# The other two edits, and two late row pairs turned and summed inside the last cross attention

## The chip, the cores and the metric

One NeuronCore of a Trainium2 chip. The metric is device time in microseconds (us) of one execution, as the median of several. TensorE (PE) does the matmuls, VectorE (DVE), ScalarE (ACT) and GpSimd (POOL) the rest, and SyncE (SP) issues all transfers between HBM and SBUF. Each engine works through its own list of instructions in order and waits on semaphores.

## The reference

A decoder layer with pre-norm, x of 4 x 512 x 1024 in f32:

```python
x = x + self_attention(layernorm(x))           # 32 heads of 32, 16 KV heads, causal, with biases
x = x + cross_attention(layernorm(x), ctx)     # 32 heads, 8 KV heads, 64 context rows, a mask
xn = layernorm(x)
g, u = xn @ Wg.T, xn @ Wu.T                    # NF4 codes x absmax per 64 columns, 3584 x 1024
x = x + (silu(g) * u) @ Wd.T                   # NF4 as well, 1024 x 3584
```

## The kernel before

Matmuls work on f16 pairs: a value is a high part and a low part, and a product takes three matmuls (high x high, high x low, low x high). ScalarE writes the high (a copy), VectorE or POOL the low (value minus high).

**Attention.** Self attention runs in steps s = -6 to 67. A step scores one block (`score`), turns and weighs another, and projects q, k or v in four pieces (`project`, L1164, L1170). Steps -6 to -3 only project; step -2 is the first that also scores, and needs masks which POOL writes (L1060 to L1077) and counts in `selected`. Projections go through HBM (`nat_parts`) into `q_rows` and `k_rows`. The last batch's cross attention comes by itself (`last_cross`), 16 iterations n and a tail. An iteration is a chain: PE score (L1259), VectorE mask and maximum (L1671, L1675), POOL shift (L996), ScalarE exponential (L1440), PE turn (L1266), ScalarE high (L1444), VectorE low (L1679), PE weigh (L1278), VectorE output `x_out` (L1684, L1688), POOL add (L1003).

**The FFN's input.** It is 1024 columns x 2048 rows, worked on as eight row pairs j. Pairs 0 to 3 are made during self attention. For each late pair 4 to 7: SP loads (L292), VectorE takes statistics (L301 to L307), POOL the root (L312), VectorE normalises (`normal`, L321), PE turns in two phases (L336), ScalarE copies (L345), VectorE makes five sums (`sum_turned`, L359), and ScalarE and POOL cut seven highs (L370) and seven lows (L376, counted in `x_low`).

**Gate and up.** Quadrants are multiplied by a seven-product scheme (Strassen and Winograd): M1 to M7 of 12 matmuls each make a *set* (L2081), 56 sets s = 2k + nb for k = 0 to 27. Set 0 can run on the first pairs, set 1 needs all of them (`x_low` 56). During half step (k, nb) the other engines dequantise two tiles of k + 1's weights: ScalarE draws codes and their comparisons (`draw`, L425 in part 0, L428), VectorE looks them up (L438, six times) and subtracts (L449), POOL scales (L455), sums (L465) and cuts lows (L482), ScalarE cuts highs (L478). The hidden values go through HBM in f16 pairs.

**Down.** 28 chunks of two tiles each, in slabs of 3, 4, 7, 7 and 7 chunks; each slab passes over all 16 rows of 128, with six matmuls 128x512 per chunk and row (L2114). `add_down` (L2339) adds a row's two banks to y. A down tile is drawn, looked up and scaled as above, then `down_high` (ScalarE, L2143) and `down_low` (POOL, L1988) cut it. The six tiles of slab 0 are made in k = 27's half steps, three each, those of slab s + 1 during slab s (`tiles_in`), spread over its 16 rows. Three pairs of PSUM banks take turns for the rows. SP loads h rows (L1935, seven slots) and, at the slab's start, the 16 rows of y (L1940).

## Time and profile before

| | us |
|---|---|
| median of 3 runs | 2695.02 (2693.35 to 2696.4) |
| span of the profiled execution | 2699.7 |
| PE busy in it | 2469.7 (91%) |
| DVE busy | 1786.3 (66%) |
| ACT busy | 1631.8 (60%) |
| POOL busy | 1525.4 (57%) |

The profile describes one execution, whose span is 4.7 us above the median of the runs; durations below are its own. Line numbers are those of the kernel before. A row "10.77 <-POOL" says that the engine stood idle for 10.77 us ahead of this instruction and that POOL ended it.

### The profile page before, as it was taken

To read this page: it belongs to the slowest core of one execution; us is meant where nothing else is said; L and a number is where in the kernel's file an instruction comes from. 1 tells how busy PE (TensorE), PEld (TensorE's weight loads), DVE (VectorE), ACT (ScalarE), POOL (GpSimd) and SP (SyncE) were. 2 spreads that over 40 slices of the span, in tenths; PEclk is the share of its full clock that TensorE was granted. 3 is DMA by queue.
4 is the path that set the end of the run, shared out by engine and by line. 5 is a ranking of instruction groups with operands and counts; after the bars stand their busy time and mean duration, and the time that the engine had idled before them with its cause. 6 is when DMAs were issued, how large, how long until landed. Compare 5 with 4: busy or idle time off the path is not lost.

```text
span 2699.7 us, 48588 instructions
## 1 busy us (share of the span) xinstructions
PE 2469.7 (91%) x17864; PEld 1343.9 (50%) x17864; DVE 1786.3 (66%) x3004; ACT 1631.8 (60%) x2998; POOL 1525.4 (57%) x1360
## 2 busy tenths in 40 slices
PE   5899999999985557999999999999997897999999
PEld 3576777777764333444444444444443333444444
DVE  5566678767777766777777777777777666555511
ACT  3466666666665436777777777777775565544400
POOL 2356677777769456777777777777774222222200
PEclk9999999999987568999999999999998998999999
DMA  6243443433232211322222222222325433333232
GB/s 199 81 141 108 119 130 105 121 108 107 80 103 87 77 48 43 90 90 88 89 91 82 83 90 83 89 86 86 93 86 202 139 106 114 105 99 100 93 103 76
DMA packets 225885, 271.11 MB, mean 100 GB/s; under 512 B 37616, under 2 KB 148720, under 8 KB 225648
## 3 DMA queue, kind: packets, MB, share of 16 engines
q1 hardware_dynamic: 225648, 268.00, 31.7%
q8 instruction: 143, 2.34, 0.4%
q14 instruction: 94, 0.77, 0.1%
HBM read 192.81 MB, written 73.40 MB: 99 GB/s over the span
## 4 chain that ended last, share of the span: by engine, by line
PE 49%; DVE 3%; issue 3%; POOL 3%; ACT 2%; DMA 1%; SPq 0%; DVEq 0%; POOLq 0%; ACTq 0%
PE ps L2081 33%; PE ps L2114 16%; POOL xT L455 1%; DVE ps L438 1%; ACT w_l L428 1%; DVE p L438 1%; DVE xT L449 1%; DMA proj<-in_codes 1%; ACT ps L425 1%; POOL xn L1993 0%; POOL q_rows L482 0%; SPq L1940 0%; DMA h_parts<-xn 0%; POOL p L465 0%; POOL x_row L1999 0%
## 5 line engine op out<-in xcount | busy, mean ns | idle before, releaser
L438 DVE TENSOR_TENSOR ps<-ps,w_l 128x512 f32<-128x512 f32 x672 | 443.0, 693 | 283.7 <-ACT w_l L428 157.3
L455 POOL TENSOR_TENSOR xT<-xT,nat 128x512 f32<-128x512 f32 x164 | 208.9, 1274 | 530.5 <-DVE xT L449 530.5
L982 POOL TENSOR_TENSOR arena<-p,arena 128x512 f16<-128x512 f32 x320 | 371.1, 1168 | 225.8 <-ACT arena L1436 225.1
L428 ACT ACTIVATE w_l<-proj 128x512 f32<-128x512 int32 x672 | 397.8, 616 | 9.4 <-DMA proj<-in_codes 9.4
L1428 ACT ACTIVATE p<-ps 128x512 f32<-128x512 f32 x320 | 191.1, 597 | 265.7 <-PE ps L1223 260.8
L1640 DVE TENSOR_REDUCE block_max<-ps 128x4 f32<-128x512 f32 x320 | 219.2, 688 | 182.5 <-PE ps L1194 179.9
L2081 PE MATMUL ps<-arena,q_rows 128*128 128x512 f16 x1344 | 296.4, 380 | 10.5 <-POOL arena L376 10.3
L425 ACT ACTIVATE ps<-proj,small 128x512 f32<-128x512 int32 x336 | 216.9, 677 | 90.2 <-DVE xT L449 87.2
L2339 DVE SCALAR_TENSOR_TENSOR arena<-ps,arena 128x1024 f32<-128x1024 f32 x70 | 84.9, 1221 | 241.2 <-PE ps L2114 230.0
L1164 PE MATMUL ps<-xT,w_h 128*128 128x512 f16 x720 | 222.0, 391 | 10.8 <-POOL arena L1077 10.8
L2081 PEld LDWEIGHTS ps<-arena,q_rows 128*128 128x128 f16 x1344 | 131.8, 98 | 170.7 <-POOL arena L376 10.8
L1436 ACT ACTIVATE arena<-p 128x512 f16<-128x512 f32 x320 | 192.0, 620 | 0.0
L2081 PE MATMUL ps<-w_h,q_rows 128*128 128x512 f16 x840 | 191.5, 383 | 0.0
L465 POOL TENSOR_TENSOR p<-xT 128x512 f32<-128x512 f32 x135 | 171.9, 1274 | 10.3
L2114 PE MATMUL ps<-w_h,w_l 128*128 128x512 f16 x672 | 150.6, 381 | 9.8 <-POOL w_h L1988 6.3
L1192 PE MATMUL ps<-k_rows,q_rows 96*128 96x512 f16 (+3 forms) x512 | 136.6, 306 | 21.0 <-DMA q_rows<-nat_parts 11.0
L2081 PE MATMUL ps<-arena,k_rows 128*128 128x512 f16 x672 | 152.0, 379 | 1.4 <-DVE x_row L2294 1.4
L1221 PE MATMUL ps<-q_rows,k_rows 97*128 97x512 f16 (+3 forms) x512 | 136.8, 306 | 13.6 <-DVE arena L1679 9.5
L1164 PE MATMUL ps<-xT,w_l 128*128 128x512 f16 x360 | 140.5, 390 | 0.0
L2081 PEld LDWEIGHTS ps<-w_h,q_rows 128*128 128x128 f16 x840 | 83.2, 99 | 100.9 <-issue 4.3
L2154 ACT ACTIVATE x_row<-ps 128x512 f32<-128x512 f32 x110 | 64.7, 588 | 105.4 <-DVE xT L2265 34.7
L449 DVE TENSOR_TENSOR xT<-ps,p 128x512 f32<-128x512 f32 x164 | 113.4, 692 | 5.7
(246 smaller groups left out, 5951.4 us busy)
## 6 DMA issues: line engine op xcount, KB each, us to landing
proj<-in_codes SPq DMA_DIRECT2D x168, 256.0 KB, 2.6
nat<-in_scales SPq DMA_DIRECT2D x336, 128.0 KB, 2.9
h_parts<-xn SPq DMA_DIRECT2D x112, 256.0 KB, 2.3
nat_parts<-nat SPq DMA_DIRECT2D x48, 256.0 KB, 2.0
q_rows<-nat_parts SPq DMA_DIRECT2D x96, 128.0 KB, 2.7
w_l<-h_parts SPq DMA_DIRECT2D x21, 448.0 KB, 4.1
x_unit<-in_x SPq DMA_DIRECT2D x64, 128.0 KB, 2.7
x<-x_unit SPq DMA_DIRECT2D x64, 128.0 KB, 2.4
```

The source lines that it names most:

```text
L425: op = self.nc.scalar.activation(out, self.t.codes[:, t % 2, :], ACT.Relu, scale=slope, bias=(self.t.above, self.t.below)[side])
L428: op = self.nc.scalar.activation(out, self.t.codes[:, t % 2, :], ACT.Copy, scale=slope, bias=intercept)
L438: self.nc.vector.tensor_tensor(other if n == self.LUT - 2 else held, held, other, ALU.max).then_inc(self.lut, 1)
L455: self.nc.gpsimd.tensor_tensor(self.quarter(t), self.quarter(t), self.t.scales[:, t % 2, :], ALU.mult)\
L465: self.nc.gpsimd.tensor_tensor(self.w_sum(k, m), self.quarter(4 * k + a), self.quarter(4 * k + b), op)\
L982: nc.gpsimd.tensor_tensor(p_l[:, n % 2, k, :], p32[:, f % 3, :], p_h[:, n % 2, k, :], ALU.subtract).then_inc(p_low, 1)
L1164: mm = nc.tensor.matmul(dst[:, :], w[:, c, cols], xT[:, :, half, c, :], start=(c == 0 and m == 0), stop=(c == CT - 1 and m == 2))
L1428: nc.scalar.activation(p32[:, f % 3, :], bank[T_BANK + T_OF[f % CHUNKS]][:, :], ACT.Exp, scale=SELF_SCALE).then_inc(t_exp, 1)
L1436: nc.scalar.activation(p_h[:, n % 2, k, :], p32[:, f % 3, :], ACT.Copy).then_inc(p_high, 1)
L1640: nc.vector.reduce_max(block_max[:, n % PAIRS, k, :], bank[S_BANK + S_OF[k]][:, :].rearrange("p (a n) -> p a n", n=P), AX_X)\
L2081: mm = nc.tensor.matmul(out, t.fw[k % 2][m][:, w, P * c:P * c + P], feed.x_of(nb, m, x, c), start=(n == 0 and m in (M1, M2, M3, M6)), stop ...
L2114: mm = nc.tensor.matmul(ps[:, 2 * (idx % 3) + half, :], hT[:, n, h, :], d[:, w, HALF * half:HALF * half + HALF], start=(n == 0 and m == 0) ...
```

## The change

It has four parts.

1. *Startup.* The wait for all masks moves from ahead of step -6 to ahead of step -2, and step -2's four projection pieces are issued ahead of its scores.
2. *Late pairs 4 and 5* are handled inside `last_cross`: pair 4's statistics in n = 9, normal 10, turn and sums 11 and 12, highs and lows from 12 to 15; pair 5's statistics in 13, normal 14, turn and sums 15 and 16, highs and lows behind. Sums now lie in the tails of `k_rows` and `q_rows` for all late pairs, copies in `x1T`; the first cut of k = 1's weights therefore waits for all 56 lows. PE's turn of iteration n - 1 comes before the weigh of n - 2.
3. *Down tiles.* Two of them (`EARLY`, chunk 0) are made as a third tile in half steps (23,0) and (25,0); k = 27 makes two in each half step. Later slabs' tiles are spread over 14 rows. ScalarE writes a tile's high between the two parts of the next tile's draws.
4. *The start of the down matmul.* h rows 0 to 3 are loaded before the last half step; y is loaded one row at a time beside h and the tiles.

```diff
@@ tensor, attention
-        pe.wait_ge(selected, 8)
         for s in range(FROM, TO):
+            if s == -2:
+                pe.wait_ge(selected, 8)
             step(s)
...
+            if s == -2:
+                for piece in range(4):
+                    project(kind_in(s), piece)
             for k in range(CHUNKS):
...
-                if kind_in(s) is not None and k < 4:
+                if kind_in(s) is not None and k < 4 and s != -2:
                     project(kind_in(s), k)
@@ last_cross
+                if 1 <= n <= NX:
+                    if n >= 2:
+                        pe.wait_ge(x_low, x - 1)
+                    x_turn(x - 1, LT_BANK, p32[:, (x - 1) % 3, :])
                 if n >= 2:
...
                     x_weigh(x - 2, LO_BANK, p_h[:, x % 2, 0, :], p_l[:, x % 2, 0, :])
-                if 1 <= n <= NX:
-                    if n >= 2:
-                        pe.wait_ge(x_low, x - 1)
-                    x_turn(x - 1, LT_BANK, p32[:, (x - 1) % 3, :])
...
+                if n in (11, 12, 15, 16):
+                    feed.turn(pe, 4 + n // 15, (n + 1) % 2 if n >= 15 else n - 11)
@@ scalar, last cross
+            if n in (11, 15):
+                for half in range(2):
+                    feed.copy_turned(act, 4 + n // 15, half)
...
+            for high in {12: (0, 1, 2), 13: (3, 4), 14: (5, 6)}.get(n, ()):
+                feed.x_cut_high(act, 4, high)
@@ gpsimd, last cross
+            for low in {12: (0, 1), 13: (2, 3), 14: (4,), 15: (5, 6)}.get(n, ()):
+                feed.x_cut_low(pool, 4, low)
@@ gpsimd, feed forward
-        x_lows(4, range(4))
         feed.root(pool, 6)
-        x_lows(4, range(4, 7))
-        x_lows(5, range(7))
+        x_lows(5, range(4))
+        feed.root(pool, 7)
+        x_lows(5, range(4, 7))
+        x_lows(6, range(3))
         join(0)
-        feed.root(pool, 7)
-        x_lows(6, range(7))
+        x_lows(6, range(3, 7))
         x_lows(7, range(7))
@@ cut_high
+        if k == 1:
+            act.wait_ge(self.x_low, 56)
@@ tiles
+    EARLY = (NK - 5, NK - 3)
...
         if k + 1 < NK:
-            return [4 * (k + 1) + 2 * nb, 4 * (k + 1) + 2 * nb + 1]
-        return [WT + 3 * nb + n for n in range(3)]
+            early = [feed.down_tile(feed.EARLY.index(k))] if nb == 0 and k in feed.EARLY else []
+            return [feed.weight_tile(k + 1, 2 * nb), feed.weight_tile(k + 1, 2 * nb + 1)] + early
+        return [feed.down_tile(len(feed.EARLY) + 2 * nb + n) for n in range(2)]
@@ sync, down
+                if (k, nb) == (NK - 1, 1):
+                    for idx in range(4):
+                        load_h(idx)
...
+        for n in range(4):
+            load_y(n)
+            store_h(8 * GROUPS - 4 + n)
+            if 4 + n < H_SLOTS:
+                load_h(4 + n)
         for idx in range(NI):
+            if idx + 4 < RT:
+                if idx + 4 == 14:
+                    sp.wait_ge(h_low, 8 * GROUPS)
+                load_y(idx + 4)
@@ scalar, down
-        for idx in range(NI):
-            for at in tiles_in(idx):
-                feed.draw(act, at, 0)
-                feed.draw(act, at, 1)
-                down_high(at)
...
+        for before, at in zip(LATE, LATE[1:]):
+            feed.draw(act, at, 0)
+            down_high(before)
+            feed.draw(act, at, 1)
+        down_high(LATE[-1])
```

Where rows move, in order. First, VectorE in the last cross attention (after the change L349 is `sum_turned`; L1671 to L1688 and L1709 to L1726 are an iteration's softmax and output, L301 to L307 and L294 to L300 statistics). Before, in the last iterations:

```order
L1671 TENSOR_TENSOR p<-ps,arena 128x512
L1675 TENSOR_REDUCE s_top<-p 128x8
L1679 TENSOR_TENSOR arena<-ps,arena 128x512
L1684 RECIPROCAL rx_sum<-ps 128x8
L1688 TENSOR_TENSOR arena<-ps,rx_sum 128x256
L1679 TENSOR_TENSOR arena<-ps,arena 128x512
L1684 RECIPROCAL rx_sum<-ps 128x8
L1688 TENSOR_TENSOR arena<-ps,rx_sum 128x256
L301 BN_STATS arena<-xn 128x6 x2
L304 BN_AGGR f_moments<-arena 128x2
L307 TENSOR_SCALAR f_moments<-f_moments 128x1
```

After, in n = 12 and 13:

```order
L1722 RECIPROCAL rx_sum<-ps 128x8
L1726 TENSOR_TENSOR arena<-ps,rx_sum 128x256
L349 TENSOR_TENSOR k_rows<-ps,x1T 128x512 x3
L349 TENSOR_TENSOR q_rows<-ps,x1T 128x512
L1709 TENSOR_TENSOR p<-ps,arena 128x512
L1713 TENSOR_REDUCE s_top<-p 128x8
L1717 TENSOR_TENSOR arena<-ps,arena 128x512
L1722 RECIPROCAL rx_sum<-ps 128x8
L1726 TENSOR_TENSOR arena<-ps,rx_sum 128x256
L294 BN_STATS arena<-xn 128x6 x2
L297 BN_AGGR f_moments<-arena 128x2
L300 TENSOR_SCALAR f_moments<-f_moments 128x1
```

Four of pair 4's sums now stand ahead of an iteration's softmax, where there were none. Pair 5's statistics (the last three rows) come behind the softmax of n = 13 and no longer between the last low part and the last output.

Second, ScalarE in the late tiles (L425 and L428 draw; after the change L436 and L439; L2143 and L2199 are `down_high`). Before:

```order
L2143 ACTIVATE w_h<-xT 128x512
L428 ACTIVATE w_l<-proj 128x512 x2
L425 ACTIVATE ps<-proj,small 128x512 x2
L428 ACTIVATE w_l<-proj 128x512
L428 ACTIVATE nat<-proj 128x512
L428 ACTIVATE w_l<-proj 128x512
L428 ACTIVATE p<-proj 128x512
L2143 ACTIVATE w_h<-xT 128x512
```

After:

```order
L439 ACTIVATE w_l<-proj 128x512 x2
L436 ACTIVATE ps<-proj,small 128x512 x2
L2199 ACTIVATE w_h<-xT 128x512
L439 ACTIVATE w_l<-proj 128x512
L439 ACTIVATE nat<-proj 128x512
L439 ACTIVATE w_l<-proj 128x512
L439 ACTIVATE p<-proj 128x512
```

The high now comes after the first four draws of the next tile, and no longer between two tiles.

Third, SP at the end of the gate and up matmuls (L1920, after the change L1967, stores the hidden values; L1935 and L1982 load h rows; L1940 and L1987 load y). Before:

```order
L411 DMA nat<-in_scales 64x512 x2
L406 DMA proj<-in_codes 128x512
L411 DMA nat<-in_scales 64x512 x2
L1935 DMA w_l<-h_parts 128x768 x3
L1920 DMA h_parts<-xn 128x4x256 x4
L1940 DMA arena<-x 128x1024 x4
L1935 DMA k_rows<-h_parts 128x768 x2
L1935 DMA x1T<-h_parts 128x768
L1935 DMA x_row<-h_parts 128x768
L1940 DMA arena<-x 128x1024 x10
L1940 DMA xT<-x 128x1024 x2
L406 DMA proj<-in_codes 128x512
```

After:

```order
L417 DMA proj<-in_codes 128x512
L422 DMA nat<-in_scales 64x512 x2
L1967 DMA h_parts<-xn 128x4x256 x2
L417 DMA proj<-in_codes 128x512
L422 DMA nat<-in_scales 64x512 x2
L1987 DMA arena<-x 128x1024
L1967 DMA h_parts<-xn 128x4x256
L1982 DMA k_rows<-h_parts 128x768
L1987 DMA arena<-x 128x1024
L1967 DMA h_parts<-xn 128x4x256
L1982 DMA k_rows<-h_parts 128x768
L1987 DMA arena<-x 128x1024
```

The h loads come first, and a single row of y stands between a store and an h load, where four and then ten were sent at once.

## Rows read from the trace of the kernel before

**Rows 1.** Stretches: PE, PEld, DVE, ACT, POOL busy (instructions), PEclk, DMA share, GB/s.
```profile
0.00:110.00 110.00, 72.45 (x535) 43.11 (x536) 58.01 (x91) 39.15 (x56) 26.20 (x37) 0.94 0.49 159
...
780.00:990.14 210.14, 118.95 (x1160) 89.80 (x1157) 159.16 (x309) 105.15 (x195) 142.81 (x141) 0.66 0.23 71
990.14:1048.20 58.06, 33.03 (x148) 18.92 (x149) 32.91 (x54) 28.63 (x51) 36.69 (x33) 0.76 0.08 28
1048.20:2052.72 1004.52, 1000.71 (x4620) 451.11 (x4620) 740.76 (x1165) 765.52 (x1419) 730.27 (x602) 1.00 0.28 87
2052.72:2148.16 95.44, 70.56 (x307) 30.11 (x307) 63.44 (x88) 47.93 (x87) 30.28 (x25) 0.91 0.60 202
2148.16:2265.72 117.56, 94.34 (x403) 40.24 (x403) 79.57 (x114) 69.59 (x127) 33.98 (x28) 0.92 0.35 107
```

**Rows 2.** Startup's timelines: start, duration, engine, line, [idle before <-releaser].
```profile
32.74 1.03 PE L1164 MATMUL ps<-xT,w_h 128*128 128x512 f16 x2 [10.77 <-POOL arena L1077]
...
40.37 0.59 PE L1164 MATMUL ps<-xT,w_h 128*128 128x512 f16 x2
...
50.73 0.28 PE L1170 MATMUL ps<-w_h,xT 128*128 128x128 f16 x2
...
62.41 0.61 PE L1192 MATMUL ps<-k_rows,q_rows 96*128 96x512 f16 x1 [4.59 <-DMA q_rows<-nat_parts]
...
22.64 0.69 DVE L1594 TENSOR_TENSOR xT<-ps,xT 128x512 f16<-128x512 f32 x1 [0.16 <-ACT xT L1369]
...
24.72 2.45 DVE L1546 SCALAR_TENSOR_TENSOR w_l<-x_row,w_h 128x1024 f16<-128x1024 f32 x2
```

**Rows 3.** Timeline of ScalarE in the last cross attention.
```profile
967.74 0.63 ACT L1440 ACTIVATE p<-p 128x512 f32<-128x512 f32 x1 [0.47 <-POOL p L996]
...
971.53 0.63 ACT L1440 ACTIVATE p<-p 128x512 f32<-128x512 f32 x1 [0.47 <-POOL p L996]
...
978.11 0.63 ACT L1440 ACTIVATE p<-p 128x512 f32<-128x512 f32 x1 [3.25 <-POOL p L996]
```

**Rows 4.** Timelines of the FFN's head.
```profile
995.79 0.32 SPq L292 DMA_DIRECT2D xn<-x  x1
...
990.36 1.09 PE L336 MATMUL ps<-ident,xn 128*128 128x128 f32 x4 [3.14 <-issue]
...
991.53 0.80 DVE L321 TENSOR_SCALAR x_unit<-x_unit,f_moments 128x1024 f32<-128x1024 f32 x1
...
1016.70 1.64 DVE L321 TENSOR_SCALAR x_unit<-x_unit,f_moments 128x1024 f32<-128x1024 f32 x1
...
1007.27 12.09 POOL L376 TENSOR_TENSOR arena<-arena 128x512 f16<-128x512 f32 x10
...
1048.20 14.72 PE L2081 MATMUL ps<-arena,q_rows 128*128 128x512 f16 x60 [10.30 <-POOL arena L376]
...
1067.53 1.17 POOL L482 TENSOR_TENSOR q_rows<-p,q_rows 128x512 f16<-128x512 f32 x1
```

**Rows 5.** Timelines of the start of the down matmul.
```profile
2065.59 13.31 PE L2114 MATMUL ps<-q_rows,w_l 128*128 128x512 f16 x54 [12.87 <-issue]
...
2075.11 1.23 DVE L2339 SCALAR_TENSOR_TENSOR arena<-ps,arena 128x1024 f32<-128x1024 f32 x1 [11.15 <-DMA arena<-x]
```

**Rows 6.** Timelines of slab 1 of the down matmul.
```profile
2168.34 1.91 DVE L438 TENSOR_TENSOR ps<-ps,w_l 128x512 f32<-128x512 f32 x3 [2.59 <-ACT ps L425]
...
2166.06 0.63 ACT L2143 ACTIVATE w_h<-xT 128x512 f16<-128x512 f32 x1 [3.17 <-POOL xT L455]
...
2173.04 15.70 PE L2114 MATMUL ps<-w_h,w_l 128*128 128x512 f16 x72
```

**Rows 7.** Timelines of the last k's two half steps.
```profile
2039.48 2.75 PE L2081 MATMUL ps<-arena,k_rows 128*128 128x512 f16 x12 [1.35 <-DVE x_row L2294]
...
2055.35 1.91 DVE L438 TENSOR_TENSOR ps<-ps,w_l 128x512 f32<-128x512 f32 x3 [0.76 <-ACT ps L425]
```

**Rows 8.** TensorE's waits, 1060 to 2045 us: total, times, longest.
```profile
PE ps L2081 <- POOL q_rows L482: 2.3, 2, 1.8
```

More of the change, by code:

```diff
@@ L441, in subtract @@
         dve.wait_ge(self.lut, self.LUT * t + self.LUT - 1)
-        k, j = t // 4, t % 4
-        if 8 <= t < self.WT + 4:
+        d = self.down_index(t)
+        early = len(self.EARLY)
+        k, j = self.weight_index(t) if d is None else (self.NK, d % 4)
+        if d is None and k >= 2 or d is not None and early <= d < early + 4:
             dve.wait_ge(self.w_summed, 5 * (k - 1) + (3, 5, 4, 5)[j])
@@ L446, in subtract @@
                 dve.wait_ge(self.w_low, 7 * (k - 1) + (None, 2, 4)[j])
-        elif t >= self.WT + 4:
-            dve.wait_ge(self.d_low, t - 4 - self.WT + 1)
+        elif d is not None and 1 <= d < early:
+            dve.wait_ge(self.d_low, d)
+        elif d is not None and d >= early + 4:
+            dve.wait_ge(self.d_low, d - 3)
         self.nc.vector.tensor_tensor(self.quarter(t), self.maximum(0), self.line(t, 1, 3), ALU.subtract)\
@@ L962, in _ @@
             sp.wait_ge(x2_stored[x1_slot(rt)], 16 * x1_count(B - 2, rt))
+        sp.wait_ge(ln_turned, 2 * LN_AT["cross", B - 1, 2] + 2)
+        feed.load_pair(sp, 4)
         sp.wait_ge(ln_turned, 2 * len(LN_ORDER))
-        for j in range(4, 6):
-            feed.load_pair(sp, j)
+        feed.load_pair(sp, 5)
         store_last(1)
@@ L1897, in tiles_in @@
         lo, hi = 2 * SLAB_AT[s + 1], 2 * SLAB_AT[s + 2]
-        return [WT + lo + n for n in range((hi - lo) * r // RT, (hi - lo) * (r + 1) // RT)]
+        ends = [min(hi, lo + (hi - lo) * n // (RT - 2)) for n in (r, r + 1)]
+        return [feed.down_tile(d) for d in range(*ends)]
+    LATE = [at for idx in range(NI) for at in tiles_in(idx)]
     def h_tile(i, nb, c):
@@ L2035, in half_step @@
                 down_low(tiles[0])
-                feed.scale(pool, tiles[2])
                 down_low(tiles[1])
-                down_low(tiles[2])
+            else:
+                for at in tiles[2:]:
+                    feed.scale(pool, at)
+                    down_low(at)
         def x_lows(j, ns):
@@ L2054, in _ @@
                 half_step(k, nb)
-        for n in range(8 * GROUPS - 4, 8 * GROUPS):
+        for n in range(8 * GROUPS - 4, 8 * GROUPS - 1):
             hidden_low(n)
-        for idx in range(NI):
-            for at in tiles_in(idx):
-                feed.scale(pool, at)
-                down_low(at)
+        for n, at in enumerate(LATE):
+            feed.scale(pool, at)
+            if n == 0:
+                hidden_low(8 * GROUPS - 1)
+            down_low(at)
     @block.tensor
@@ L2119, in _ @@
         rest.banks_free(pe)
-        turn(4)
         pe.wait_ge(x_low, 28)
@@ L2133, in down_high @@
         def down_high(at):
-            chunk = (at - WT) // 2
+            d = feed.down_index(at)
+            chunk = d // 2
             act.wait_ge(feed.scaled, at + 1)
-            if chunk < 3:
+            if chunk < 1:
+                pass
+            elif chunk < 3:
                 act.wait_ge(product, 7 * (NSET - 2))
@@ L2208, in half_step @@
                 down_high(tiles[0])
-                for part in range(2):
-                    feed.draw(act, tiles[2], part)
                 down_high(tiles[1])
-                down_high(tiles[2])
+            else:
+                for at in tiles[2:]:
+                    feed.draw(act, at, 0)
+                    feed.draw(act, at, 1)
+                    down_high(at)
             if s >= 1 and k % 2 == 0:
@@ L2226, in _ @@
         act.wait_ge(w_low, 7)
-        copies(4)
-        highs(4, range(2))
+        highs(5, range(3))
         copy(0, 0)
-        highs(4, range(2, 7))
+        highs(5, range(3, 7))
         copy(0, 1)
-        copies(5)
-        highs(5, range(7))
         copies(6)
@@ L2236, in _ @@
         copies(7)
+        highs(7, range(7))
         rest.scores_done(act)
@@ L2323, in half_step @@
             feed.subtract(dve, tiles[1])
-            if k + 1 == NK:
-                look_up(tiles[2])
+            for at in tiles[2:]:
+                look_up(at)
             if s >= 1:
```

151 lines of the change are left out of this document (81 added, 70 removed).

## The prediction

> **What bounds the kernel now.** I read the table of stretches first [rows 1]: where is TensorE not busy? From 1048.20 to 2052.72 us (sets 1 to 55 of the FFN) it is busy 1000.71 of 1004.52 us. It is the bound there, and an edit can only cost time. It stands still for 37.6 us before 110, for 91.2 in the last cross attention (780 to 990.14), for 25.0 in the FFN's head (to 1048.20), and for 24.9 and 23.2 in the first two slabs of the down matmul (2052.72 to 2265.72). A gain has to come out of these gaps.
>
> Second, the timelines at the gaps, for what each wait is charged to:
> - Startup [rows 2]. The first projection starts at 32.74, after 10.77 us charged to a POOL memset. What it computes with was there long before: the last activations (VectorE L1594, 22.64 + 0.69 = 23.3) and the fourth low part of the weights (L1546, 27.2). Later a score waits 4.59 us for q_rows.
> - Last cross attention [rows 3]. The exponentials of two steps are 3.8 us apart where VectorE has only the softmax (967.74, 971.53), and 6.6 where it also has pair 4's statistics (971.53, 978.11).
> - The FFN's head [rows 4]. 58.06 us pass from the end of the last cross attention (990.14) to set 1 (1048.20). POOL decides: ten of its lows run from 1007.27, and set 1 waits 10.30 us for its last.
> - Down matmul [rows 5, 6]. Set 55 ends at 2052.72, the first down matmul starts at 2065.59 after 12.87 us, and the first add waits 11.15 us for a row of y that was sent in a burst. Slab 1 advances by VectorE's dequantisation, 14 tiles in its 117.56 us [rows 1], some 8 us each. VectorE waits 2.59 us of it for ScalarE's draw (L425, ahead of 2168.34), and ScalarE, ahead of its high (L2143), 3.17 us for POOL's scale.
>
> **Term 1, startup.** Without the wait for the masks, the first projection starts at 23.4 instead of 32.74, -9.3. It took 7.63 us (to 40.37 [rows 2]), at first on the lower clock. Started at 23.4, its last quarter comes after 28, when the fourth low part (27.2) is there, so nothing new waits. And the four pieces of the next projection now stand ahead of the first scores. From the end of q2's matmuls (50.73, two projections after 40.37, so 5.18 each) to the score that waits for q_rows (62.41) a chain of 11.7 us runs through bias, stores and SP; TensorE filled it with v and then stood still for 4.59. With 5.2 us of projection in that place the wait is covered. What is lost is that these pieces no longer fill later waits for VectorE's maxima. I take -4.2 of the 4.6: **-13.5** (-10 to -15).
>
> **Term 2, last cross attention and head.** The last cross attention ends later. VectorE gets ten sums of 128x512 f32; three operations of that shape take 1.91 us [rows 6], so 6.4 us. TensorE gets four turn phases, each of two groups like that of 1.09 us at 990.36 [rows 4], 8 us in all, where it is busy 118.95 of 210.14 us. Against that TensorE now turns step n-1 before it weighs step n-2, so the exponentials' chain no longer has the weighing in it: some 0.5 us of a clean step of 3.8, over twelve steps 6 at most. Pair 5's statistics no longer stand right ahead of the last x_out, four sums do. I take +4.4 (+2 to +8).
>
> After it, the head. Pair 6's load is issued at 995.79, when pair 4 has been turned (990.36 and on) [rows 4]; now pair 4 was turned before, and only the last store is ahead, so the rows land some 5 us after the end of attention instead of 9. Then some 3 us of statistics (6.6 - 3.8 in [rows 3], rounded up), 0.7 of root, and on POOL 21 lows at 1.21 (12.09 for ten) and 2 us of join and root: 5 + 3 + 0.7 + 25.4 + 2 = 36.1, so some 37 instead of 58.06, -21. TensorE's own 33.03 us there fall by the four phases, so it isn't the bound. But k = 1's weights don't come earlier by as much: the two silus now stand ahead of ScalarE's first draw for them, and its first cut waits for all 56 lows, since the sums lie in its room. POOL's M1 low (1067.53 + 1.17) was done just when set 2 began, 20 us after set 1. A lag of 3 us against little slack is a stall of 2 to 3. Sum: 4.4 - 21 + 2.6 = **-14** (-8 to -20).
>
> VectorE's L321 takes 0.80 us beside an idle POOL and 1.64 beside POOL's lows [rows 4]. On this the Trainium skill (SBUF — State Buffer, "Who interferes with whom") says that a `tensor_scalar` in a two-port mode and GpSimd exclude each other from a shared pair of ports for a whole instruction. By that page the two normals left in the head, beside 21 uninterrupted lows, would delay either engine by up to 1 us each, so the sum would be some 2 us worse; the trace agrees in kind, and the range has room for it.
>
> **Term 3, two down tiles early.** Half steps (23,0) and (25,0) get a third tile: on VectorE six lookups and a subtract, 0.64 each by the 1.91 for three, 4.5 us; on ScalarE eight draws and a high at 0.53 to 0.63, 4.9; on POOL a scale and a low, 2.4. In [rows 1] a set of 18.15 us has 13.4 us of VectorE, 13.8 of ScalarE and 13.2 of POOL. With the third tile ScalarE has 18.7, over the set, before it waits for POOL's scale ahead of the high; the next set takes the lag back. What reaches TensorE: the same third tile in (27,0) cost it 1.35 [rows 7], where no further weights followed. In the middle there is none to spare at an even k: the only waits of these sets are two for POOL's low, the longer 1.8 [rows 8]. From 1.35 to 5 a tile: 3.5 each, +7 (+3 to +12), less the 1.35 in (27,0), where there are two tiles now: **+5.6**.
>
> **Term 4, down matmul.** In slab 1, 72 matmuls take 15.70 us [rows 6], 0.216 each. A row is 18 of them in slab 0 (3.89) and 24 in slab 1 (5.18): 16 x 3.89 + 16 x 5.18 = 145.1 us if nothing waits, against 2265.72 - 2052.72 = 213.0 now. What could wait:
> - The start. Four h loads are issued before set 55 ends, and the last tile of chunk 2 has four tiles ahead of it in the last k and not six. I take 3 us, with the first rows' waits.
> - y. One row of 512 KB per 3.89 us instead of 16 at once; with a tile's 512 KB per 6.8 us and 192 KB of h per row that is some 260 GB/s by the issued sizes. The stretch that holds the burst has a mean of 202 at a share of 0.60 [rows 1]. It fits, though not by much.
> - The cycle. A tile's high now stands between the two halves of the next tile's draws, so ScalarE doesn't wait for VectorE and POOL ahead of them. VectorE's 4.5, one add (1.2) and what lies between its subtract and the next L438 by way of L425 (0.76 at 2055.35 [rows 7]), partly filled by the add, give 5.4 to 6.0. Slab 1 has 14 tiles in 14 rows of 5.18: at 5.7 VectorE falls behind by 14 x 0.5 = 7 us, and TensorE may be two rows, 10.4 us less the add, ahead of the adds, since three pairs of banks take turns. It just fits; from 6.2 it costs 14 x 1.0 - 9 = 5 us and more. Slab 0's eight tiles have 54 us, 6.8 each.
> - The start of slab 2. Its last tile is ready at 14 x 5.9 + 3 = 86 us into slab 1, and needed at 82.9 + 7.8 = 90.7.
>
> 213.0 - 145.1 - 3 = **-65** (-58 to -67).
>
> **Sum.** -13.5 - 14 + 5.6 - 65 = -86.9. The profiled execution's span, 2699.7, is 4.7 above the median of 2695.02. The changed kernel's span would be 2613, its median **2608**.
>
> **Rivals.**
> - *The tile cycle stays.* If something other than ScalarE's order makes the 8 us, slab 1 keeps its 117.56 in place of 82.9: 2643. For it: the draw of L425 needs the bank that VectorE's subtract frees, before as after. Against it: in (27,1), where the last tile's draws stood ahead of the high, VectorE waited only 0.76 for L425 [rows 7], not 2.59. 0.07.
> - *The last cross attention gives back what the head saves.* If sums, turns and copies each hold up a step's chain, five more steps take 6.6 instead of 3.8 (+14), and POOL's seven lows among its shifts and adds cost half of their 8.4 (+4.2): 14 more than my +4.4, term 2 is nothing, 2622. 0.15.
> - *The early tiles cost more,* as ScalarE is over its set: 5 to 6 a tile and an echo in the next k, +6, 2614. 0.1. That they are free: 2601, 0.1.
> - *The other side.* The weight pipeline falls out of step for good: set 1 comes before k = 1's weights, and since an even k has no slack [rows 8], each of the 54 sets behind it waits. The gain of 87 us is 1.6 us a set, so from 19.75 instead of 18.15 us a set on the kernel is slower; at 2 us a set it takes 2608 + 108 = 2716. Against it: all three engines have over 4 us of idle time in a set, so a lag of 3 us is gone after one. 0.02.
> - *Transfers collide in slab 0.* If y, h and codes at 260 GB/s land late and each wait like the 11.15 us of [rows 5] comes back once: +11, 2619. 0.08.
>
> **Chances and range.** My forecast, with all terms within their bounds: 0.48. The best ends of all terms together give 2595, the worst 2630. Rivals below 2636 are held too; out are the kept cycle, the other side and mixtures of several. Range 2592 to 2636. A measurement of this kernel tells a difference of about 0.2% (5.4 us) from none; only the other side and what lies near it get there: faster 0.97, same 0.01, slower 0.02.
>
> **What the profile of the changed kernel would show.** The first projection at 23 to 24 us, with no wait for a memset. The last x_out at 979 to 985 (13.5 earlier, 2 to 8 later), set 1 some 37 us behind it. From set 1 to set 55, 1004 us and 5 to 15 more, with the waits at set 2 and behind (23,0) and (25,0). The first down matmul within 3 us of the last product, L438 starts 5.4 to 6 apart in slab 1, slab 2 some 148 us after set 55. I am wrong if L438 starts stay 8 apart, if the down matmul's start waits for a transfer, if set 1 waits over 12 us for the lows, or if the last x_out is at 990 or later.

## The result and the profile after

The changed kernel takes 2626.11 us (median of 4 runs, 2620.46 to 2634.21), the kernel before 2695.71 (4 runs, 2693.35 to 2698.97): a ratio of 0.9735, with a 95% interval of 0.971 to 0.9761. That is 69.6 us faster; forecast were 87, and a time of 2608 in a range of 2592 to 2636. The profiled execution has a span of 2629.2 us against 2699.7. Of five executions of the same kernel in a later session (experiment 2) one took 11067 us; it is left out of all figures.

First the stretches of the changed kernel's profile: to the last output of the attention, to set 1, to the last product, slab 0, slab 1 with the first 36 matmuls of slab 2 (up to the point at which the kernel before stood at 2265.72), and the rest. All but one of the ends are the same points in the work as in [rows 1]. The exception is the start of slab 1:

```profile
767.00:989.56 222.56, 125.27 (x1276) 97.92 (x1274) 173.63 (x330) 113.39 (x211) 156.60 (x153) 0.67 0.24 73
989.56:1028.27 38.71, 26.80 (x117) 13.79 (x117) 22.94 (x38) 21.54 (x38) 28.56 (x25) 0.82 0.12 41
1028.27:2044.01 1015.74, 1001.69 (x4621) 450.60 (x4622) 750.44 (x1181) 770.43 (x1429) 733.50 (x606) 1.00 0.28 88
2044.01:2106.57 62.56, 62.33 (x289) 28.06 (x288) 54.46 (x75) 46.12 (x83) 26.11 (x22) 1.00 0.83 270
2106.57:2197.30 90.73, 90.73 (x421) 41.04 (x420) 84.82 (x122) 74.42 (x133) 35.67 (x30) 1.00 0.51 154
2197.30:2629.20 431.90, 427.57 (x1982) 193.63 (x1979) 174.31 (x237) 138.06 (x241) 66.86 (x56) 1.00 0.30 96
```

The 2148.16 of [rows 1] is not the start of slab 1, but the end of a wait of 6.26 us behind its first 18 matmuls. Cut at the slabs' own ends, the kernel before has:

```profile
2052.72:2137.84 85.12, 66.50 (x289) 28.43 (x289) 56.85 (x80) 41.04 (x74) 26.47 (x22) 0.90 0.63 213
2137.84:2247.26 109.42, 90.45 (x384) 38.47 (x384) 75.13 (x107) 64.63 (x117) 31.56 (x27) 0.94 0.34 107
2247.26:2265.72 18.46, 7.95 (x37) 3.45 (x37) 11.03 (x16) 11.86 (x22) 6.22 (x6) 0.84 0.36 113
```

Against [rows 1] the four parts of the difference, and the forecast of each:

| stretch | before | after | difference | forecast |
|---|---|---|---|---|
| start to the last output of the attention | 990.14 | 989.56 | -0.6 | -9.1 |
| to set 1 | 58.06 | 38.71 | -19.4 | -21 |
| set 1 to the last product of set 55 | 1004.52 | 1015.74 | +11.2 | +8.2 (set 2 2.6, early tiles 5.6) |
| down matmul to the end | 646.98 | 585.19 | -61.8 | -65 |
| span | 2699.7 | 2629.2 | -70.5 | -86.9 |

The waits are gone where they were largest. In the two slabs TensorE is busy for 62.33 of 62.56 and 90.73 of 90.73 us, and on the higher clock level throughout (1.00, where [rows 1] has 0.91 and 0.92). VectorE's tile in slab 1, and ScalarE around its high (L449 looks up, L2395 adds to y; L438 and L2339 before):

```profile
2125.13 1.29 DVE L449 TENSOR_TENSOR ps<-ps,w_l 128x512 f32<-128x512 f32 x2
2126.72 0.70 DVE L449 TENSOR_TENSOR ps<-ps,w_l 128x512 f32<-128x512 f32 x1 [0.30 <-ACT w_l L439]
...
2129.85 1.21 DVE L2395 SCALAR_TENSOR_TENSOR arena<-ps,arena 128x1024 f32<-128x1024 f32 x1
2130.98 1.29 DVE L449 TENSOR_TENSOR ps<-ps,w_l 128x512 f32<-128x512 f32 x2
```

```profile
2124.11 1.30 ACT L436 ACTIVATE ps<-proj,small 128x512 f32<-128x512 int32 x2 [0.68 <-DVE xT L464]
2125.54 0.63 ACT L2199 ACTIVATE w_h<-xT 128x512 f16<-128x512 f32 x1
2126.07 0.61 ACT L439 ACTIVATE w_l<-proj 128x512 f32<-128x512 int32 x1
```

From 2125.13 to 2130.98 are 5.85 us a tile, with the add in it. ScalarE's high (L2199) waits for nobody; [rows 6] had 3.17 us ahead of it.

The first stretch is the surprise. Startup, on VectorE and POOL:

```profile
18.54 7.18 DVE L1626 TENSOR_SCALAR xn<-x_row,mean_var,roots 128x1024 f32<-128x1024 f32 x1 [0.66 <-POOL roots L995]
...
29.06 0.69 DVE L1632 TENSOR_TENSOR xT<-ps,xT 128x512 f16<-128x512 f32 x1 [0.16 <-ACT xT L1396]
```

```profile
18.88 5.80 POOL L1079 MEMSET arena<- 128x2080 f16 x4
```

```profile
26.45 1.94 PE L1145 MATMUL ps<-ident,xn 128*128 128x128 f32 x8 [8.72 <-DVE xT L1632]
29.86 1.01 PE L1185 MATMUL ps<-xT,w_h 128*128 128x512 f16 x2 [1.46 <-DVE xT L1632]
```

VectorE's fourth normalisation (L1626), 0.81 us for the other three, takes 7.18 and ends at 25.72, behind POOL's four long memsets (18.88 to 24.68) and the short one that follows them (to 25.17). All that follows is 6.4 us later: the transposes start at 26.45 (20.03 before), and the first projection at 29.86, not at 23.4 as forecast. In the profile of the kernel before VectorE isn't held up, and a memset is:

```profile
18.47 0.81 DVE L1588 TENSOR_SCALAR xn<-x_row,mean_var,roots 128x1024 f32<-128x1024 f32 x1 [0.66 <-POOL roots L976]
```

```profile
18.38 0.21 POOL L1060 MEMSET ident_b<- 128x128 bf16 x1
18.52 0.20 POOL L1060 MEMSET mask_qk<- 128x128 bf16 x1
18.67 0.76 POOL L1060 MEMSET mask_kq<- 128x128 bf16 x1
```

In both profiles the normalisation starts 0.09 us behind the first of eight memsets (18.45 in the changed kernel), so the start times don't tell which engine will be held up. In the kernel before, the 10.77 us of waiting for the masks are more than such a loss of 6.4 us, and would have hidden it.

### The profile page after: what moved, and what is told of

The parts are those of the page before. It is cut to its first block, busy times and chain, and to the rows that moved or that the text cites. A ratio compares the mean times of both kernels' runs of the same rounds, so it can differ in the third digit from the quotient of the medians.

```text
span 2629.2 us, 48595 instructions
## 1 busy us (share of the span) xinstructions
PE 2450.1 (93%) x17864; PEld 1340.4 (51%) x17864; DVE 1793.5 (68%) x3004; ACT 1638.1 (62%) x2998; POOL 1523.6 (58%) x1360
## 4 chain that ended last, share of the span: by engine, by line
PE 50%; POOL 3%; issue 2%; DVE 2%; ACT 1%; DMA 1%; SPq 0%; DVEq 0%; ACTq 0%; POOLq 0%
PE ps L2135 29%; PE ps L2168 21%; POOL q_rows L500 1%; POOL xT L470 1%; POOL p L481 1%; POOL xn L2042 1%; DVE p L449 0%; ACT w_l L439 0%; DVE ps L449 0%; DMA h_parts<-xn 0%; POOL x_row L2048 0%; DVE xT L464 0%; DMA proj<-in_codes 0%; ACT q_rows L496 0%; ACT ps L436 0%
## 5 line engine op out<-in xcount | busy, mean ns | idle before, releaser
L449 DVE TENSOR_TENSOR ps<-ps,w_l 128x512 f32<-128x512 f32 x672 | 444.2, 693 | 237.4 <-ACT w_l L439 162.3
L439 ACT ACTIVATE w_l<-proj 128x512 f32<-128x512 int32 x672 | 398.8, 618 | 64.2 <-DVE ps L449 52.2
L436 ACT ACTIVATE ps<-proj,small 128x512 f32<-128x512 int32 x336 | 217.7, 680 | 170.7 <-DVE xT L464 167.7
L2395 DVE SCALAR_TENSOR_TENSOR arena<-ps,arena 128x1024 f32<-128x1024 f32 x70 | 85.1, 1221 | 211.4 <-PE ps L2168 208.9
L481 POOL TENSOR_TENSOR p<-xT 128x512 f32<-128x512 f32 x135 | 171.8, 1272 | 10.3
L1213 PE MATMUL ps<-k_rows,q_rows 96*128 96x512 f16 (+3 forms) x512 | 136.1, 305 | 16.3 <-DVE block_max L1678 9.0
L2135 PE MATMUL ps<-w_l,q_rows 128*128 128x512 f16 x504 | 113.5, 379 | 4.7 <-POOL q_rows L500 4.7
```

Source lines behind the costliest of these rows:

```text
L436: op = self.nc.scalar.activation(out, self.t.codes[:, t % 2, :], ACT.Relu, scale=slope, bias=(self.t.above, self.t.below)[side])
L439: op = self.nc.scalar.activation(out, self.t.codes[:, t % 2, :], ACT.Copy, scale=slope, bias=intercept)
L449: self.nc.vector.tensor_tensor(other if n == self.LUT - 2 else held, held, other, ALU.max).then_inc(self.lut, 1)
L481: self.nc.gpsimd.tensor_tensor(self.w_sum(k, m), one, other, op)\
L2135: mm = nc.tensor.matmul(out, t.fw[k % 2][m][:, w, P * c:P * c + P], feed.x_of(nb, m, x, c), start=(n == 0 and m in (M1, M2, M3, M6)), stop ...
```

## The experiments

All are compared by the same four stretches, which hardly change from run to run but for the first: in six profiles (the changed kernel twice, experiments 1, 4, 5 and 6), set 1 comes 38.6 to 38.7 us behind the attention and the sets take 1015.7 to 1016.4 us. By the *lead* of a kernel I mean how much earlier than in the profile of the kernel before an event comes; it compares single executions. "On the late memsets" means that a kernel also has the edit of experiment 1, and is compared with it.

**1. The memsets wait for the normalisation.**

```diff
+        pool.wait_ge(ln_xn, 4)
         for buf in cleared:
             nc.gpsimd.memset(buf[:], 0.0).then_inc(zeroed, 1)
```

> The changed kernel, but POOL begins its eight clearing memsets only when VectorE has normalised the fourth row tile. In the changed kernel's profile that fourth normalisation took 7.18 us instead of 0.81, for as long as the four long memsets (5.80 us), and the four runs fall into 2620 to 2621 and 2631 to 2634. Theory 1 (the normalisation and the memsets race, and where VectorE comes second it stands still for the memsets): 0.81 us again, first projection at 23 to 24 us, all runs at 2620 to 2624, some 6 to 10 us below the slow ones. Rival (the spread comes from transfers or the clock, and the masks now come 0.5 us later): runs still spread over 10 us, median 2626.

Measured: 2621.31 us (2618.34 to 2624.49), ratio 0.9711 (0.9694 to 0.9727).

```profile
18.52 0.81 DVE L1627 TENSOR_SCALAR xn<-x_row,mean_var,roots 128x1024 f32<-128x1024 f32 x1 [0.66 <-POOL roots L995]
```

```profile
20.08 1.94 PE L1146 MATMUL ps<-ident,xn 128*128 128x128 f32 x8 [2.36 <-DVE xT L1633]
23.48 1.01 PE L1186 MATMUL ps<-xT,w_h 128*128 128x512 f16 x2 [1.46 <-DVE xT L1633]
```

The normalisation takes 0.81 us again, the first projection starts at 23.48 as forecast, and the attention ends at 979.43 (10.1 us earlier than in the changed kernel; at the first cross attention mask the lead is 17.1 us, where the changed kernel has 9.6). The other stretches are the same to 0.3 us. That the memsets make the 7.18 us is shown by this; that they explain the whole spread is not, as the next two show.

**2. The changed kernel once more.**

> The changed kernel itself once more. Theory 1 (its fourth normalisation loses the race with the memsets in most executions): 7.18 us again in the profile and a median of 2625 to 2629, 5 to 7 us above the kernels with the late memsets in this call after their other edits are taken off (2620 for the one without further edits). Rival (the race is even and the 7.18 us of the first profile were chance, the spread lies in the self attention's transfers): 0.81 us, median 2621 to 2624.

Measured: four executions from 2622.0 to 2626.88 us, whose median is 2625.3; ratio 0.9721 (0.97 to 0.9742).

```profile
18.57 0.95 DVE L1626 TENSOR_SCALAR xn<-x_row,mean_var,roots 128x1024 f32<-128x1024 f32 x1 [0.66 <-POOL roots L995]
```

The profiled execution (span 2620.2) has the normalisation at 0.95 us, and its attention ends at 980.06. So the race is open: of the five profiles of kernels with the startup part and early memsets, four show 7.18 us and one 0.95. Neither expectation fits whole: the profile is the rival's, the median the first theory's. The kernel with late memsets is 4 to 5 us faster by the medians, but runs of both spread by 5 us or more, and only the profiled executions tell what their normalisation did. More of the spread arises in the self attention: in some profiles the lead falls there by 1 to 3 us at a batch change, in others it stays or grows. TensorE's waits for `xT<-xT_parts`, 4.1 us in all before, are 5.7 in the changed kernel's first profile, but 5.7 in that of experiment 1 as well, which holds its lead; so they don't settle it.

**3. Startup alone,** on the kernel before.

```diff
-        pe.wait_ge(selected, 8)
         for s in range(FROM, TO):
+            if s == -2:
+                pe.wait_ge(selected, 8)
             step(s)
...
+            if s == -2:
+                for piece in range(4):
+                    project(kind_in(s), piece)
```

(ScalarE gets a wait for the masks ahead of step -2 as well, as it has in the changed kernel.)

> The kernel before with the startup part alone (mask wait ahead of step -2, the four projection pieces ahead of its scores). Theory 1: the full effect where the memsets don't stand in the way is -16 us, where they do -10; it is passed on to the end less some 3 us lost at transfers in the self attention, so 2682 to 2690. Rival (the last cross attention or its transfers swallow the lead): 2693 or more. My forecast's term was -13.5, so 2682.

Measured: 2685.93 us (six runs, 2683.46 to 2696.13), the kernel before 2699.88 in the same session, ratio 0.995 (0.9934 to 0.9965): -14. The profiled execution has the stall of 7.18 us and was the slowest of the six, with a lead of 8.2 us at the first cross attention mask and 5.0 at the attention's end. At that mask the four profiles with 7.18 us have leads of 8.2 to 14.7 us, and the eight with a short normalisation 14.7 to 19.3, and the medians give 14 us for the part. The lead that is left at the attention's end goes through to the end of the kernel (5.3 us in the span).

**4. TensorE's order in the last cross attention undone** (the weigh of n - 2 ahead of the turn of n - 1; nothing else).

> The changed kernel with TensorE's old order in the last cross attention: the weigh of n - 2 ahead of the turn of n - 1. Theory 1 (the swap brought nothing, as the first eight periods, 6.3 us, are the same in both profiles): 2626 within the runs' spread, the last output of the attention at most 1 us later. Rival (my forecast's 0.5 us a step): +5 to 6 us, 2632.

Measured: 2626.99 us (2623.04 to 2635.65), 0.9736 (0.9715 to 0.9757). From the 58th to the 64th softmax of the attention it loses 6.1 us against the kernel before, the changed kernel 6.4. To the attention's end it loses 5.8, the changed kernel 5.5, so with the pairs in these steps the swap brings 0.3 us, within what other profiles with the new order show (5.5 to 5.9), and my 0.5 us a step is refuted. Without them it brings a little more: experiment 9 has the new order and no pair work there, and gains 1.3 us on the kernel before.

**5. ScalarE's order in the late tiles undone.**

```diff
-        for before, at in zip(LATE, LATE[1:]):
-            feed.draw(act, at, 0)
-            down_high(before)
-            feed.draw(act, at, 1)
-        down_high(LATE[-1])
+        down_high(LATE[0])
+        for at in LATE[1:]:
+            feed.draw(act, at, 0)
+            feed.draw(act, at, 1)
+            down_high(at)
```

> The changed kernel with ScalarE's old order in the late tiles: a tile's high ahead of both parts of the next tile's draws. Theory 1 (this order alone made the 8 us tile cycle): the starts of L438's counterpart are 8.1 us apart in slab 1 again, and slab 1 takes 114 to 118 us instead of 83: +30 to +35, some 2658. Rival (the spread of tiles and y loads did as much): +5 to +15, 2631 to 2641.

Measured: 2664.98 us (2664.61 to 2666.08), 0.9873 (0.9857 to 0.9889). The last stretch takes 622.8 us in place of 585.2, +37.6; nothing else changes.

```profile
2128.05 1.91 DVE L449 TENSOR_TENSOR ps<-ps,w_l 128x512 f32<-128x512 f32 x3 [2.60 <-ACT ps L436]
...
2136.20 1.91 DVE L449 TENSOR_TENSOR ps<-ps,w_l 128x512 f32<-128x512 f32 x3 [2.60 <-ACT ps L436]
```

```profile
PE ps L2168 <- DVE arena L2395: 27.2, 15, 4.1
```

8.15 us a tile, with the same 2.60 us ahead of L449 as in [rows 6], and 27.2 us of TensorE's waits for the adds, in 15 pieces. Where this one line stands makes more than half of the whole change's gain.

**6. Loads of h and y in the old order** (on the late memsets).

```diff
-                if (k, nb) == (NK - 1, 1):
-                    for idx in range(4):
-                        load_h(idx)
...
+        for idx in range(3):
+            load_h(idx)
...
+        for n in range(4, RT):
+            load_y(n)
```

> The late-memset kernel (2621) with the old order of loads at the down matmul: h rows only behind the last half step, four rows of y, h, then the other twelve rows of y at once. Theory 1 (the first down matmul waited for h, the first add for y and the first codes for the burst): the down matmul starts 5 to 9 us behind the last product instead of at once, and slab 0 has another 6 to 12 us of waits, total 2633 to 2641. Rival (only the start matters, since the slack of slab 0 takes the burst): +5 to +9, 2626 to 2630.

Measured: 2643.0 us (2637.53 to 2645.41), 0.9785 (0.9763 to 0.9808). The last stretch takes 605.7 us, 20.3 more than in experiment 1.

```profile
2037.37 2.41 PE L2168 MATMUL ps<-x_row,w_l 128*128 128x512 f16 x6 [4.25 <-issue]
...
2077.12 2.72 PE L2168 MATMUL ps<-x_row,w_l 128*128 128x512 f16 x6 [10.71 <-DMA w_l<-h_parts]
```

TensorE waits 4.25 us at the start (5 to 9 were expected) and 10.71 in the middle of slab 0, where a load of h stands behind the twelve rows of y, and 1.46 for an add behind that. The rest is the lower clock behind the first two waits: slab 0 has a mean granted clock of 0.90 with them, and the six matmuls at 2037.37 take 2.41 us, 1.46 in the changed kernel. With experiment 5 this makes 57.9 us of the 61.8 that the last stretch gained. The spread over 14 rows in place of 16 was not undone by itself.

**7. No early tiles** (on the late memsets; the six tiles in the last k, three in each half step).

```diff
-    EARLY = (NK - 5, NK - 3)
+    EARLY = ()
...
-        return [feed.down_tile(len(feed.EARLY) + 2 * nb + n) for n in range(2)]
+        return [feed.down_tile(3 * nb + n) for n in range(3)]
```

> The late-memset kernel (2621), with no early down tiles: all six tiles of slab 0 in the last two half steps, three each, as in the kernel before. Theory 1 (the third tile costs 4.5 us in each of the two early half steps): set 1 to set 55 takes 1006 to 1008 us instead of 1015.8, and the down matmul waits in its first row for chunk 2's last tile, some 6 to 8 us: total 2618 to 2622, so that the early tiles bring nothing. Rival (the wait at the down matmul is over 12 us, since h, stores and the last hidden parts queue behind those tiles): 2626 or more, and the early tiles earn their cost.

Measured: 2624.26 us (2620.81 to 2626.25), 0.971 (0.9695 to 0.9725). The sets take 1006.8 us (9.0 less) and the down matmul 594.8 (9.4 more):

```profile
2027.58 1.46 PE L2167 MATMUL ps<-x_row,w_l 128*128 128x512 f16 x6
2032.20 2.74 PE L2167 MATMUL ps<-q_rows,w_l 128*128 128x512 f16 x6 [3.17 <-POOL q_rows L2038]
2038.49 2.53 PE L2167 MATMUL ps<-q_rows,w_l 128*128 128x512 f16 x6 [3.55 <-POOL q_rows L2038]
```

What the early tiles save at the start of slab 0, 6.7 us of waits and the lower clock behind them, is what they cost in the sets. The two stretches together are 1601.2 us with them and 1601.6 without; most of the 3 us between the medians (2624.26 and 2621.31) is not in them, but in the attention, at whose end the profile's lead is 8.0 us, and 10.7 in experiment 1. By the sets: 47 and 48 take 20.75 and 20.99 us in the changed kernel, and 18.13 and 18.27 here, so an early tile costs 5.3 us; set 55 gives 1.6 back, as (27,0) has two tiles and not three.

**8. An early tile's work spread** (on the late memsets and the order of experiment 10).

```diff
             for at in tiles[2:]:
-                look_up(at)
+                feed.greater(dve, at, range(3))
...
                     right_sum(s, n)
+            for at in tiles[2:]:
+                feed.greater(dve, at, range(3, LUT - 1))
+                feed.subtract(dve, at)
```

> The kernel with the late memsets and the new order in the head (2620), and in it the early tile's work placed otherwise: VectorE does three of its six look-ups ahead of the set's right sums and the rest behind them, ScalarE writes its high behind the next half step's first draws and POOL its low behind the next scale. Theory 1 (the 4.5 us of each early tile are waits for right sums and for POOL's lows that queue behind the tile): set 1 to set 55 takes 1009 to 1011 us instead of 1015, total 2614 to 2616. Rival (the engines are simply full: 18 us of work in a set of 18.15, so TensorE waits wherever the tile is put): 1014 to 1016, total 2620.

Measured: 2625.08 us (2620.01 to 2632.12), 0.9723 (0.9699 to 0.9748); the sets take 1020.49 us, 5.5 more.

```profile
1876.99 4.33 PE L2136 MATMUL ps<-arena,k_rows 128*128 128x512 f16 x12 [2.69 <-DVE x_row L2317]
```

My theory fell, and the rival's 1014 to 1016 us was too low as well: the wait moves from the right sums (1.35) to the difference of the next set (2.69 instead of 0.95), and TensorE falls to the lower clock behind it (4.33 us for twelve matmuls, 2.75 in the changed kernel's rows, which follow).

```profile
1876.59 2.75 PE L2135 MATMUL ps<-arena,k_rows 128*128 128x512 f16 x12 [1.35 <-DVE x_row L2350]
...
1885.47 2.75 PE L2135 MATMUL ps<-arena,k_rows 128*128 128x512 f16 x12 [0.95 <-DVE x_row L2315]
...
1906.45 3.84 PE L2135 MATMUL ps<-w_l,q_rows 128*128 128x512 f16 x17 [1.84 <-POOL q_rows L500]
```

**9. Pairs 4 and 5 left in the FFN's head** (on the late memsets; the second part of the change undone but for TensorE's order, with the old homes for sums and copies).

```diff
-            if n in (9, 13):
-                feed.stat(dve, 4 + n // 13, (x_added, LATE_X + 4 * (n // 13 + 1)))
...
-                if n in (11, 12, 15, 16):
-                    feed.turn(pe, 4 + n // 15, (n + 1) % 2 if n >= 15 else n - 11)
...
+        x_lows(4, range(4))
         feed.root(pool, 6)
```

> The late-memset kernel (2621), with the second part of the change undone but for TensorE's order: pairs 4 and 5 are made in the FFN's head, with the kernel before's homes for sums and copies; startup, down tiles and down loads as changed. Theory 1: the attention ends 6.3 us earlier, the head takes 58 us again instead of 38.7, and the 3.8 us wait at set 2 goes: 2621 - 6.3 + 19.4 - 3.8 = 2630. So this part is worth 9 us of the 70, where my forecast gave it 14. Rival (the attention doesn't become shorter, for its length came from TensorE's order or the startup): 2636.

Measured: 2634.92 us (2630.86 to 2637.25), 0.975 (0.9734 to 0.9765). Head 58.85 us and not 38.71 (20.1 more), sets 1013.87 (1.9 less), and from the 58th softmax to the attention's end 1.3 us less than the kernel before, where the late-memset kernel has 5.5 more (6.8 less). So this part is worth 20.1 - 6.8 - 1.9 = 11.4 us; by the medians 13.6, which is near the rival's time, though the attention did become shorter. The profiled executions differ by 16.1 us; 5.4 of these arise in the self attention, where the lead at the 58th softmax is 10.9 us here and 16.3 in experiment 1.

**10. The head in another order** (on the late memsets).

```diff
-        feed.root(pool, 6)
-        x_lows(5, range(4))
-        feed.root(pool, 7)
-        x_lows(5, range(4, 7))
+        x_lows(5, range(7))
+        feed.root(pool, 6)
+        feed.root(pool, 7)
...
-            if n in (1, 3):
-                turn(6 + n // 2)
+            if n in (2, 3):
+                turn(4 + n)
```

> The late-memset kernel (2621), with two orders changed in the FFN's head: POOL cuts all seven lows of pair 5 ahead of the roots of pairs 6 and 7, and TensorE computes M3 ahead of pair 6's turn. In the changed kernel POOL stands still for 8.8 us ahead of the root of pair 6 while pair 5's highs are there, and TensorE for 6.4 us ahead of that turn. Theory 1 (both are order, not work): set 1 starts 33 to 35 us behind the last output of the attention instead of 38.7, total 2616 to 2619. Rival (pair 6's load, 6.2 us behind the attention, and VectorE's work on it set the end whatever POOL does first; or set 2 waits that much longer for its weights): the sum of both stretches is the same within 1 us, 2621.

Measured: 2619.83 us (2614.9 to 2623.31), 0.9689 (0.9671 to 0.9707), the lowest median of all, though 1.5 us below experiment 1 are within the spread of either. The stretches are clearer: set 1 comes 36.16 us behind the attention, 2.5 less (33 to 35 us were expected), and the sets take 0.8 less. The changed kernel's root of pair 6, and both roots here:

```profile
999.18 0.70 POOL L305 TENSOR_TENSOR f_moments<-f_moments,small 128x2 f32<-128x2 f32 x1 [8.80 <-DVE f_moments L300]
```

```profile
995.83 0.69 POOL L305 TENSOR_TENSOR f_moments<-f_moments,small 128x2 f32<-128x2 f32 x1
1001.42 0.69 POOL L305 TENSOR_TENSOR f_moments<-f_moments,small 128x2 f32<-128x2 f32 x1 [4.90 <-DVE f_moments L300]
```

The 8.80 us of waiting ahead of the first root are used for pair 5's lows, but 4.90 of them come back ahead of the second, whose statistics (pair 7's) stand behind pair 6's load and normals on VectorE. Both theories had a part.

**11. Pair work in the gap behind the maximum** (on the late memsets).

```diff
                 x_soft(x, LS_BANK, p32[:, x % 3, :])
+            if n in (10, 14):
+                feed.stat(dve, 4 + n // 14, (x_added, LATE_X + 4 * (n // 14 + 1)))
+            if n in (11, 15):
+                feed.normal(dve, 4 + n // 15)
...
             if 1 <= n <= NX:
                 x_low_part(x - 1, LT_BANK, p_h[:, (x - 1) % 2, 0, :], p_l[:, (x - 1) % 2, 0, :])
```

> The late-memset kernel (2621), with VectorE's work on pairs 4 and 5 in the last cross attention moved behind the next step's maximum (where VectorE waits 1.2 us or more for ScalarE in each step) and not ahead of its mask, and the root, highs and lows moved by one step accordingly. Theory 1 (the 6.3 us that the last cross attention became longer come from the place ahead of the softmax, where each us is on the chain): most of it goes, the attention ends 3 to 5 us earlier, 2616 to 2618. Rival (the chain runs through POOL and TensorE too, which carry the lows and turns; or pair 4's lows come too late and hold up pair 5): no gain, 2621 to 2626.

Measured: 2624.91 us (2618.87 to 2626.3), 0.971 (0.9693 to 0.9727). Between the 58th and the 64th softmax it loses 5.1 us against the kernel before where the late-memset kernel loses 6.4, but from there to the attention's end it loses 4.1 more, where that one gains 0.8. In all it loses 9.1 us, and that one 5.5. So this other place is no better, and in so far the rival holds; as the root, highs and lows moved by a step too, the place on VectorE by itself was not tested.

## Why the forecast was off

The direction, the order of the terms and the range held; the size was 17 us too large. That the total stayed in the range owes something to chance too, since errors of both signs met in the sum. By the steps of the prediction:

- *Term 1, startup, "nothing new waits".* That sentence failed in the profiled execution. I had read when the fourth normalisation ended (in the row at 22.64 behind it) in one execution, and taken it as given. With the mask wait gone, a race with POOL's memsets lies open: 7.18 us for 0.81. Where it is won, the first projection starts at 23.48 (forecast 23.4) and the lead is 17.1 us (forecast 13.5). The wait for q_rows wasn't covered quite as I took it: 1.28 of its 4.59 us are left, 3.3 gained for 4.2. I had not counted the rest. Up to the first cross attention mask, for the same 3000 matmuls, TensorE's idle time falls by 13.9 us (44.66 to 30.78), which is 9.3 at the start, these 3.3 and 1.3 of other waits; its busy time falls by 3.2 (263.19 to 259.96), since less of the work comes on the lower clock behind waits (mean granted clock 0.96 before, 0.97 here). In the first profile 9.6 were left, of which the self attention lost 3.5 more.
- *Term 2, "I take +4.4" for the last cross attention.* Measured +5.5; within the bounds, but by two errors that cancel, which is luck. The credit for TensorE's order (6 us at most) was 1.3 without the pairs and 0.3 with them (experiments 9 and 4), and the debit for sums and turns (14.4) was 6.8 (experiment 9). *"Some 37"* for the head: 38.71. Pair 6 landed 6.2 us behind the attention and not 5, its root was done 10.3 us behind it and not 8.7, and the second root waited another 1.21. My sum had all 21 lows behind that root and took this order as given; I had not asked what could stand ahead of it. POOL stood still for 8.80 us, with highs of pair 5 ready to be worked on (experiment 10). *"A stall of 2 to 3"*: of this size, but not where I had it nor for what. Set 2 waits for nothing, and POOL's M1 low is in time. The stall is in set 1, ahead of its sixth product:

```profile
1045.19 4.98 PE L2135 MATMUL ps<-arena,q_rows 128*128 128x512 f16 x15 [3.76 <-DVE x_row L2315]
```

L2315 reads the bank that this product is added into, and stands behind a tile's look-ups on VectorE, which had waited 2.48 us for ScalarE's draws. On balance the sets lose 1.9 us by it (experiment 9), since the first 60 matmuls of set 1 take 13.16 us where [rows 4] has 14.72 behind the longer wait.
- *Term 3, "3.5 each".* 5.3 each, above my upper bound of 5, less 1.6 in (27,0): 9.0 in all for my 5.6 (experiment 7). It is what the rival "the early tiles cost more" says, with its echo in the next k: TensorE waits 1.35 and 0.95 us in set 47, and 0.41 and 1.84 in set 48. I had given it 0.1. The one other place for the work that was tried didn't help (experiment 8). What I had not asked is what they save: 9.4 us at the down matmul's start, so on balance 0.4.
- *Term 4, "against 2265.72 - 2052.72 = 213.0 now".* This step was wrong by 7.8 us: at 2265.72 the kernel before had done 36 matmuls of slab 2's first row, so the work in the 213.0 is 145.1 + 7.8 = 152.9, and 60 us is all that could be won there. Won were 59.7, since nothing of the 3 us for the start came true (the first down matmul runs at 2044.01, right behind the last product), and another 2.1 in the later rows, 61.8 in all. Both ends of what I called slab 1 were ends of waits: its 117.56 us begin 18 matmuls into it and end 36 into slab 2, where 10.51 us are a wait for that slab's tile. Slab 1 itself took 109.42, and takes 83.00 now. A check was at hand: TensorE's idle time in the two rows of [rows 1] is 48.1 us, and the rest of the 60 is the lower clock (0.91 and 0.92 where the changed kernel has 1.00). The cycle, 5.4 to 6.0 forecast, is 5.85, and it fits as reckoned: slab 1 has no wait. The rival "the tile cycle stays" is out, as the order on ScalarE alone decides the cycle: 37.6 us.

The other side didn't show: between set 1 and the early tiles the only wait over 0.3 us is one of 0.84 in set 44, where the kernel before has 0.52. The sum of the measured parts is -0.6 - 19.4 + 11.2 - 61.8 = -70.6, which is the -70.5 of the spans but for rounding.

Left open: why the last cross attention grows by 6.8 us with the pairs in it, and not by more or less. The lead falls by 3.3 us at the step of pair 4's statistics, 1.5 at its normals, 1.2 and 1.1 at its turn and sums, but moving them behind the maximum (experiment 11) only moves the loss. Taking single parts out was not tried. Nor is it settled what makes the self attention lose up to 3 us at a batch change in some executions, nor what decides the race at the start.

## What to carry to other kernels

- Add up idle time and clock level of a stretch before you promise more than that. A boundary taken at the end of a wait has work of the next stage in front of it; count the instructions on both sides.
- If an engine's order puts its own wait for the past (a high of this tile) ahead of its work for the next one (draws), the three engines take turns instead of overlapping. Ask for each instruction whether something behind it was ready; here one such swap gave 37.6 us.
- Where a wait is removed, look for what it hid: two instructions that start within a tenth of a microsecond may hold each other up either way, and one profile shows one of the ways. And work that is taken from a late place and put into a full stretch may cost all that it saves (the early tiles: 9.0 paid for 9.4).

## What the runs showed of the hardware

In the six profiles in which POOL's memsets aren't held back (the kernel before, the changed kernel twice, experiments 3, 4 and 5), VectorE's `tensor_scalar` of 128x1024 f32 starts 0.08 to 0.09 us behind the first of eight memsets. In four of them it takes 7.18 us and ends some 0.55 us behind the last memset. In the fifth it takes 0.95 us and in the sixth 0.81, and there a memset is held up: 2.37 us for 1.83 (experiment 2), 0.76 for 0.20 (the kernel before). With the memsets behind it, it takes 0.81 in all seven profiles. VectorE's `tensor_tensor` of 128x512 (0.67 to 0.69 us) and `scalar_tensor_tensor` of 128x1024 (1.21 to 1.23) were not slowed beside memsets.

This agrees with the Trainium skill (SBUF — State Buffer, "Who interferes with whom": the shared pair of ports goes to whoever issues first, for the whole instruction, and the other engine is blocked fully), in that one of the two engines stands still. I had weighed it at 1 us for one instruction; in four of these six profiles it lasted over all eight memsets.

A wait of TensorE of 2.69 us is followed by twelve matmuls in 4.33 us instead of 2.75, so it costs another 1.6 (experiment 8). Behind a wait of 1.35 us the twelve took 2.75.
